# Batch attention with 64x64 value-sum tiles and halved GpSimd products, and a new order on the way into the experts

## The chip, the core and the metric

The kernel runs on one core of a Trainium2 chip. The metric is the device time of one execution in microseconds. The core's engines are PE (TensorE, matmuls; PEld is its weight load), DVE (VectorE), ACT (ScalarE), POOL (GpSimd) and SP (SyncE, which here only issues transfers). Each runs its own instructions in order, and they wait for each other on semaphores.

## The reference, cut to what matters

The program is a chain of eight layers on x (8 samples, 256 positions, 256 features). The change lies in the fourth, `L1_ffn`. It attends over the samples of one position, not over positions, and then sends each token to two of eight experts.

```python
qkv = src @ in_proj_w.T + in_proj_b          # src: 256 positions x 8 samples x 256
q, k, v = ...reshape(s_len, bsz, H, dh)      # H = 16 heads, dh = 16
scores = jnp.einsum('sbhd,tbhd->bhst', q, k) * scale
attn = jax.nn.softmax(scores, axis=-1)
ctx = jnp.einsum('bhst,tbhd->sbhd', attn, v).reshape(s_len, bsz, d)
x = _ln(src + ctx @ out_w.T + out_b, ln1_g, ln1_b)
tok = x.reshape(-1, d)
logits = tok @ gate_w.T + gate_b
probs = jax.nn.softmax(logits, axis=-1)
topv, topi = jax.lax.top_k(probs, K)         # K = 2 of E = 8 experts
...
for e in range(E):
    h = jax.nn.relu(tok @ w1[e].T + b1[e]) @ w2[e].T + b2[e]
    moe_out = moe_out + combine[:, e:e + 1] * h
return _ln(x + moe_out, ln2_g, ln2_b)
```

As the layer is called, the eight samples of a position attend to each other: for each position and head an 8x8 table.

## The kernel before, in words

The stage is called samp. Its 16 units are (sample, half of the positions): a unit u has 128 positions on the partitions, one query sample and all eight key samples (B = 8, T = 2 halves, D = 256, DH = 16, P = 128, C = 2 halves of the features). Per unit:

- POOL multiplies the query with the eight keys, 128x2048 products (`product`, line 2286 in an order with d outermost, line 2289 in the plain order).
- The 16 products of a head are summed either on DVE (`ON_DVE`, the reduction of line 2121, from SBUF) or on PE (`ON_PE`, `products_summed`, 16 matmuls with the identity on line 2374, which leaves the sums in PSUM).
- DVE takes the maximum (2125) and subtracts it (2126), ACT takes the exponent (2330), DVE sums, inverts and scales (2131, 2132, 2133: `probs`).
- DVE multiplies the values in PSUM with the shares (2140, `values`), and PE sums over the eight samples while it transposes (`values_summed`, line 2385: 16 matmuls of 128x128 with the identity). ACT copies the sum (2345).
- PE adds the residual and the projection (`projected`, 2408 and 2411); DVE measures mean and variance (2146, 2147, 2151: `measured`), POOL makes the reciprocal root (198, 201: `rstd_of`), DVE scales (2157: `normed`); PE transposes (2393, `turned`), ACT copies (2348), PE makes the gate's logits (2417, `gated`).

All engines step through one loop over `it`. In iteration `it` PE projects unit it-1, turns and gates unit it-3, sums the values of unit `it` and the products of unit it+2; POOL makes the products of unit it+2. In PE's instruction stream one f32 matmul shows as two MATMUL records.

The picks of the two experts are made in five batches of units, (0-3), (4-7), (8-10), (11-13), (14-15). For a batch DVE reads the logits (2164), picks (2176 to 2190), signals `sel_ready`; PE counts the ranks (`ranked`, 2401, 2402); DVE makes the slots (2211 to 2220, `slots`); POOL then scatters the rows of the batch to their places in DRAM (2298, two indirect transfers per unit, in the iterations of the table `SCATTERED`). Where a batch is ranked, PE first runs nine matmuls that compute nothing (`clocked`, line 1908, on bf16, 512 columns).

After the last batch DVE makes the table of groups (`counted`), SP loads the rows of the first group of 128 tokens, and the experts begin (`moe_pe`: 2509 turns the rows, 2520 is the first product, 2530 the second). POOL zeroes a buffer (674) and then asks for the weights of experts 1 and 2 (2485, 2486). Between the last units PE also makes tables of position biases for a later layer in six parts (`bias_products`, line 2097).

In rows, `L2385` is line 2385 of the kernel, and `scr<-PS,W` says what is written and read.

## Time and profile before

| | before |
|---|---|
| median of 3 runs | 1125.13 us (1124.1 to 1125.45) |
| profiled execution, its own time | 1122.43 us |
| its span in the trace | 1120.7 us |
| PE busy / DVE busy / POOL busy, of the span | 94% / 67% / 47% |
| mean granted TensorE clock | 0.986 |

The span runs from the first to the last instruction; the time of the run is 1.7 us longer. Busy shares are averages over stages that have different limits, so a stage is read from its own stretch. The granted clock is a share of 2.4 GHz: 1.0 is 2.4 GHz and 0.5 is 1.2 GHz. The stage samp runs from about 427 to 580 us, and the experts begin at 585.42 us.

### The profile page before, as it was taken

The page shows a single profiled execution, that of the slowest core. Times are in us where ns is not written, and L with a number is a line of the kernel's source. Part 1 is how long each engine was busy: PE and PEld are TensorE (multiplying, and loading weights), DVE is VectorE, ACT ScalarE, POOL GpSimd, SP SyncE. Part 2 cuts the span into 40 slices and gives each one's busy share as a digit, 9 for nine tenths or more (in the row PEclk, how much of TensorE's full clock was granted, in tenths as well). Part 3 has the DMA queues.
Part 4 walks back from the last instruction along what each step waited for, and adds up shares of the span by engine and source line. Part 5 has one row for each costly group of instructions (what it writes and reads, how often), then busy time and mean ns, then how long its engine had stood idle before and what let it go on. Part 6 is the DMA issues. An engine that isn't in the chain of part 4 may idle for free.

```text
span 1120.7 us, 23972 instructions
## 1 busy us (share of the span) xinstructions
PE 1049.6 (94%) x8906; PEld 826.1 (74%) x8906; DVE 748.5 (67%) x1698; ACT 469.1 (42%) x940; POOL 531.8 (47%) x526
## 2 busy tenths in 40 slices
PE   9999889988899999999989999999999999999896
PEld 5676656666676567999868999999998567765564
DVE  4899879999987448889842222222222899987794
ACT  2555677775565202121112222222222446654475
POOL 5645335577873214768764010000354757541464
PEclk9999999999999999999969999999999989999999
DMA  5999900002000300000147141311221200000001
GB/s 186 368 404 389 388 8 2 23 4 91 2 1 2 107 0 1 1 11 29 57 145 304 60 174 46 113 37 37 66 80 38 67 11 11 1 1 1 0 20 57
DMA packets 45137, 93.78 MB, mean 84 GB/s; under 512 B 3934, under 2 KB 19071, under 8 KB 42487
## 3 DMA queue, kind: packets, MB, share of 16 engines
q1 hardware_dynamic: 36646, 62.24, 15.7%
q0 software_dynamic: 7104, 29.14, 7.2%
q8 instruction: 59, 0.97, 0.3%
q10 hardware_dynamic: 1296, 1.18, 0.3%
q14 instruction: 32, 0.25, 0.1%
HBM read 39.02 MB, written 51.51 MB: 81 GB/s over the span
## 4 chain that ended last, share of the span: by engine, by line
PE 64%; DVE 19%; POOL 5%; ACT 5%; issue 4%; DMA 2%; POOLq 1%; PEldq 0%; DVEq 0%; ACTq 0%; SPq 0%; PEld 0%
PE PS L2520 11%; PE PS L2530 11%; PE PS L1113 4%; PE PS L2029 4%; PE PS L2385 3%; PE PS L1089 3%; PE PS L1126 3%; PE PS L1079 2%; PE PS L1908 2%; PE PS L2374 2%; PE PS L1743 2%; POOL big L695 2%; DVE scr L476 2%; PE PS L1037 1%; PE PS L970 1%
## 5 line engine op out<-in xcount | busy, mean ns | idle before, releaser
L2554 ACT ACTIVATE scr<-PS,W 128x128 f32<-128x128 f32 x148 | 53.5, 367 | 191.1 <-PE PS L2520 191.1
L2520 PEld LDWEIGHTS PS<-scr 128*128 128x128 f32 x992 | 116.5, 192 | 5.5 <-issue 1.8
L2520 PE MATMUL PS<-scr 128*128 128x128 f32 x992 | 118.7, 276 | 1.9 <-issue 1.5
L2530 PE MATMUL PS<-scr 128*128 128x256 f32 x496 | 112.2, 379 | 0.0
L2585 DVE TENSOR_SCALAR scr<-PS,W 128x128 f32<-128x128 f32 x148 | 51.2, 350 | 88.0 <-PE PS L2520 88.0
L727 POOL TENSOR_TENSOR scr<-scr,small 128x1232 f32<-128x1232 f32 x32 | 72.0, 2250 | 73.1 <-DVE small L478 73.0
L2591 DVE TENSOR_TENSOR scr<-PS,W 128x256 f32<-128x256 f32 x37 | 15.7, 425 | 127.0 <-PE PS L2530 123.1
L2530 PEld LDWEIGHTS PS<-scr 128*128 128x128 f32 x496 | 91.8, 190 | 11.2
L868 ACT ACTIVATE big<-PS 128x512 f32<-128x512 f32 x144 | 73.0, 523 | 58.7 <-PE PS L1089 58.1
L2631 POOL DMA_DIRECT2D expert_out<-scr x28 | 15.2, 544 | 161.4 <-DVE scr L2591 159.5
L1089 PE MATMUL PS<-W,scr 128*128 128x128 f32 x480 | 78.6, 284 | 9.4 <-ACT big L846 3.0
L1089 PEld LDWEIGHTS PS<-W,scr 128*128 128x128 f32 x480 | 52.2, 141 | 23.9 <-ACT big L846 4.6
L2385 PE MATMUL PS<-W,scr 128*128 128x128 f32 x512 | 61.1, 278 | 2.4 <-DVE scr L2140 2.4
L1113 PEld LDWEIGHTS PS<-scr,big 128*64 128x64 f32 x1280 | 45.2, 137 | 22.0 <-issue 20.5
L2385 PEld LDWEIGHTS PS<-W,scr 128*128 128x128 f32 x512 | 58.5, 192 | 3.4 <-DVE scr L2140 3.3
L863 ACT ACTIVATE scr<-scr 128x1232 f32<-128x1232 f32 x48 | 58.7, 1223 | 4.3 <-POOL scr L727 2.7
L1908 PE MATMUL PS<-identb 128*128 128x512 bf16 x225 | 58.5, 402 | 0.3 <-ACT big L868 0.3
L1113 PE MATMUL PS<-scr,big 128*64 128x34 f32 (+1 forms) x1280 | 56.7, 228 | 1.1 <-ACT big L868 0.9
L1126 PE MATMUL PS<-W,big 128*128 128x256 f32 x192 | 55.3, 410 | 0.5 <-ACT big L889 0.5
L695 POOL TENSOR_TENSOR big<-big,neghalf 128x32 f32<-128x32 f32 x8 | 45.5, 5687 | 15.9 <-DVE big L431 15.7
L1743 PE MATMUL PS<-big,W 64*64 64x256 f32 x768 | 47.0, 382 | 1.3 <-ACT scr L1662 1.3
L478 DVE TENSOR_REDUCE small<-scr 128x16 f32<-128x1232 f32 x32 | 45.9, 1436 | 1.1
(432 smaller groups left out, 2424.1 us busy)
## 6 DMA issues: line engine op xcount, KB each, us to landing
expert_in<-zeros SPq DMA_DIRECT2D x1, 19712.0 KB, 59.9
expert_out<-zeros SPq DMA_DIRECT2D x1, 19712.0 KB, 112.4
scr<-ew_in POOLq DMA_DIRECT2D x12, 1024.0 KB, 6.4
scr<-expert_in SPq DMA_DIRECT2D x38, 128.0 KB, 2.1
big<-ew_in POOLq DMA_DIRECT2D x4, 1024.0 KB, 8.5
expert_out<-scr POOLq DMA_DIRECT2D x28, 128.0 KB, 2.0
W<-pack SPq DMA_DIRECT2D x1, 2458.0 KB, 8.6
W<-pack SPq DMA_DIRECT2D x1, 2152.0 KB, 9.1
```

What stands on the lines that cost most here:

```text
L695: g.tensor_tensor(a_qr[j % 2], a_qvar[j % 2], neghalf[:, 0:T * H], ALU.pow).then_inc(s["qr_ready"], 1)
L727: g.tensor_tensor(sc3, sc3, a_mx[u % 3].unsqueeze(2).broadcast_to([P, H, S2]), ALU.subtract).then_inc(s["sub_ready"], 1)
L863: a.activation(a_sc[lay][u % 3], a_sc[lay][u % 3], ACT.Exp, scale=scale).then_inc(s["p_ready"], 1)
L868: a.activation(a_PT[lay][u % 2][:, 4 * g:4 * g + n, :], bank(ring_bank(lay, "p", u, g), n * P).rearrange("p (c n) -> p c n", c=n), ACT.Cop ...
L1089: ins = pe.transpose(bank(b, P, k * P), a_sc[lay][u % 3][:, at:at + P], ident)
L1113: ins = pe.matmul(PS[k:k + OUT_COLS, 6 + u % 2, at:at + n * (DH + 1)], a_PT[lay][u % 2][:, c, k:k + OUT_COLS], a_VB[lay][:, c, 0:n, u // T ...
L1126: ins = pe.matmul(bank(6 + u % 2, D, D), a_OT[lay][:, c, :], wo[:, c, :], start=(c == 0), stop=(c == C - 1))
L1743: ins = pe.matmul(PS[c * HALF:(c + 1) * HALF, conv_bank(i, p, r), 0:S], f_taps[rows, f, j, rows], f_G[rows, f, j:j + S], start=(j == 0), s ...
L1908: pe.matmul(bank(b, size, at), identb[:, :], identb[:, :].unsqueeze(1).broadcast_to([P, size // P, P]), start=True, stop=True)
L2385: ins = pe.matmul(bank(4, P, c * P), vp[:, t, c * P:(c + 1) * P], ident, start=(t == 0), stop=(t == B - 1))
L2520: ins = pe.matmul(bank(1 + f % 4, G), e_w1[slot][:, k, f * P:(f + 1) * P], e_xT[:, k, :], start=(k == 0), stop=(k == C - 1))
L2530: ins = pe.matmul(bank(5 + t, D), e_h[:, f, t * P:(t + 1) * P], e_w2[slot][:, f, :], start=(f == 0), stop=(f == FC - 1))
```

## The change

- Three more units (6, 10, 14) have their products summed on PE: `ON_PE` was the odd units from 3 on, and is now all from 3 on but 4, 8 and 12. Their sums go to bank 7 instead of 5.
- For units in `ON_PE` POOL makes the products in two halves by d, and PE starts on the first eight while the second half is made.
- `values_summed` uses 64x64 tiles: each 128x128 matmul becomes four of 64 rows, 64 weight columns and 64 moving columns; the row halves go to two banks.
- PE waits for ACT's copy of the value sum (`cT_ready`) ahead of `clocked` and `turned`, and adds the residual (`based`) ahead of that wait.
- The end of the loop, iterations 16 to 19, is written out: picks before `measured`, ranks and bias parts interleaved anew, 40 instead of 20 matmuls of `clocked` before the experts.
- SP and no longer POOL asks for expert 0's weights, and PE and ACT read the group table ahead of turning the first rows.

```diff
-        ON_PE = [u for u in range(UNITS) if u % 2 and u > 2]
+        ON_PE = [u for u in range(UNITS) if u % 4 and u > 2]
...
+            normed(UNITS - 2)
+            v.wait_ge(s["y_full"], UNITS)
+            logits_read(LAST_BATCH - 1, False)
+            picked(LAST_BATCH - 1)
+            measured(UNITS - 1)
+            v.wait_ge(s["y_full"], UNITS + 1)
+            slots(LAST_BATCH - 1, True)
+            normed(UNITS - 1)
+            shared(LAST_BATCH - 1)
...
-                    g.tensor_tensor(by_d, q.rearrange("p t (h d) -> p t h d", h=H), k.rearrange("p t (h d) -> p t h d", h=H),
-                                    ALU.mult).then_inc(s["prod_ready"], 1)
+                    q4, k4 = (m.rearrange("p t (h d) -> p t h d", h=H) for m in (q, k))
+                    for ds in (slice(0, DH // 2), slice(DH // 2, DH)):
+                        g.tensor_tensor(by_d[:, :, :, ds], q4[:, :, :, ds], k4[:, :, :, ds], ALU.mult).then_inc(s["prod_ready"], 1)
...
-                if it == UNITS:
-                    g.wait_ge(s["b_pe"], len(ON_PE))
-                    g.wait_ge(s["b_dve"], len(ON_DVE))
-                    weights_load(g, 0, 0)
...
+                    if d == DH // 2:
+                        pe.wait_ge(s["prod_ready"], u + turns(ON_PE, u))
...
-                        ins = pe.matmul(bank(4, P, c * P), vp[:, t, c * P:(c + 1) * P], ident, start=(t == 0), stop=(t == B - 1))
+                        for r in range(2):
+                            rows = slice(r * half, (r + 1) * half)
+                            for k in range(2):
+                                at = c * P + k * half
+                                ins = pe.matmul(PS[k * half:(k + 1) * half, SUM_BANKS[r], SUM_AT + c * half:SUM_AT + (c + 1) * half],
+                                                vp[rows, t, at:at + half], ident[rows, rows], start=(t == 0), stop=(t == B - 1))
...
+            turned(UNITS - 2)
+            bias_products(pe, 2, BIAS_BANKS[2])
+            gated(UNITS - 2)
+            ranked(LAST_BATCH - 1).then_inc(s["y_full"], 1)
+            bias_products(pe, 3, BIAS_BANKS[3])
+            turned(UNITS - 1)
+            gated(UNITS - 1).then_inc(s["y_full"], 1)
+            bias_products(pe, 4, BIAS_BANKS[4])
+            pe.wait_ge(s["y_taken"], turns(TAKES, UNITS))
+            ranked(LAST_BATCH).then_inc(s["y_full"], 1)
+            bias_products(pe, 5, BIAS_BANKS[5])
             pe.sem_inc(moe["xT_psum"], 1)
-            clocked(pe, 4, 20)
+            clocked(pe, 4, 40)
...
+            sp.wait_ge(samp["b_pe"], len(ON_PE))
+            sp.wait_ge(samp["b_dve"], len(ON_DVE))
+            sp.dma_start(e_slot[0][:, 0:2048], ew1_in[0]).then_inc(in_w2, 16)
+            sp.dma_start(e_slot[0][:, 2048:4096], ew2_in[0]).then_inc(in_w2, 16)
...
-            transpose_rows(0)
             pe.wait_ge(samp["slot_ready"], len(BATCHES) + 1)
-            moe_experts(pe, body)
+            moe_experts(pe, body, begin=transpose_rows)
```

On PE, before, this stands where the first batch is ranked, in iteration 7 (2385: the value sum of unit 6; 1908: `clocked`; 2393: `turned`; 2401, 2402: ranks; 2408, 2411: residual and projection):

```order
L2385 MATMUL PS<-W,scr 128x128 x15
L1908 MATMUL PS<-identb 128x512 [waits samp_xT_ready]
L1908 MATMUL PS<-identb 128x512 x8
L2393 MATMUL PS<-W,big 128x128 [waits samp_xT_ready,samp_x1_ready]
L2393 MATMUL PS<-W,big 128x128
L2401 MATMUL PS<-scr,W 128x32 [waits samp_sel_ready,samp_y_taken]
L2402 MATMUL PS<-scr,W 128x32
L2408 MATMUL PS<-big,W 128x256
L2411 MATMUL PS<-W,scr 128x256 [waits samp_cT_ready]
```

On PE, of the change, the same place (2420: the value sum, now 64 matmuls; 2429: `turned`; 2437, 2438: ranks; 2444, 2448: residual and projection):

```order
L2420 MATMUL PS<-W,scr 64x64 x63
L1908 MATMUL PS<-identb 128x512 [waits samp_xT_ready,samp_cT_ready,samp_y_taken]
L1908 MATMUL PS<-identb 128x512 x8
L2429 MATMUL PS<-W,big 128x128 [waits samp_xT_ready,samp_x1_ready]
L2429 MATMUL PS<-W,big 128x128
L2437 MATMUL PS<-scr,W 128x32 [waits samp_sel_ready]
L2438 MATMUL PS<-scr,W 128x32
L2444 MATMUL PS<-big,W 128x256
L2448 MATMUL PS<-W,scr 128x256 x2
```

The wait for `cT_ready` moved from the projection to ahead of `clocked`. On DVE, before, this is the fourth batch of picks after the last projection (2164: read the logits; 2146, 2147, 2151: `measured` of unit 15; 2176 and on: the picks; 2157: `normed`):

```order
L2164 TENSOR_TENSOR scr<-PS,W 128x24 [waits samp_y_full]
L2146 BN_STATS scr<-PS 128x6 [waits dve_chain]
L2147 BN_AGGR scr<-scr 128x2 [waits dve_chain]
L2151 SCALAR_TENSOR_TENSOR scr<-PS,scr,W 128x256 [waits samp_x1_ready,samp_var_ready]
L2176 MAX scr<-scr 128x8 x3
...
L2190 TENSOR_TENSOR scr<-scr 128x8 [waits dve_chain] x3
L2199 TENSOR_REDUCE scr<-scr 128x3 [waits samp_texp_ready,samp_sel_ready]
...
L2157 SCALAR_TENSOR_TENSOR big<-scr,W 128x256 [waits samp_y_taken,samp_rstd_ready,dve_chain]
L2211 TENSOR_TENSOR scr<-scr,PS 128x48 [waits samp_y_full]
```

On DVE, of the change, the same batch (2167: read the logits; 2179 to 2193: the picks; 2149 to 2154: `measured`; 2214 to 2223: the slots; 2160: `normed`):

```order
L2167 TENSOR_TENSOR scr<-PS,W 128x24 [waits samp_y_full]
L2179 MAX scr<-scr 128x8 [waits dve_chain]
...
L2193 TENSOR_TENSOR scr<-scr 128x8 [waits dve_chain] x3
L2149 BN_STATS scr<-PS 128x6 [waits samp_sel_ready]
L2150 BN_AGGR scr<-scr 128x2 [waits dve_chain]
L2154 SCALAR_TENSOR_TENSOR scr<-PS,scr,W 128x256 [waits samp_x1_ready,samp_var_ready]
L2214 TENSOR_TENSOR scr<-scr,PS 128x48 [waits samp_y_full]
...
L2223 CAST SLOT<-scr 128x6 [waits dve_chain]
L2160 SCALAR_TENSOR_TENSOR big<-scr,W 128x256 [waits samp_y_taken,samp_rstd_ready]
```

`measured` moved behind the picks, and `normed` and the shares behind the slots.

## Rows read from the trace of the kernel before

**Rows 1.** Four stretches: length, busy PE, PEld, DVE, ACT, POOL, clock, DMA share, GB/s.

```profile
441.00:493.50 52.50, 51.98 (x419) 49.26 (x420) 45.28 (x102) 8.92 (x24) 34.80 (x21) 1.00 0.00 1
493.50:541.00 47.50, 45.11 (x356) 42.12 (x354) 43.75 (x84) 5.65 (x17) 41.61 (x26) 1.00 0.08 29
541.00:560.70 19.70, 19.65 (x146) 17.44 (x147) 14.70 (x48) 2.80 (x9) 13.37 (x17) 1.00 0.19 68
560.70:579.80 19.10, 16.11 (x75) 14.43 (x74) 11.45 (x75) 2.88 (x8) 12.67 (x15) 0.56 0.51 187
```

**Rows 2.** PE in order of time, one iteration; start us, us.

```profile
524.43 3.74 PE L2374 MATMUL PS<-scr,W 128*128 128x128 f32 x32
529.89 3.82 PE L2385 MATMUL PS<-W,scr 128*128 128x128 f32 x32
533.54 0.43 PE L2393 MATMUL PS<-W,big 128*128 128x128 f32 x2
```

**Rows 3.** POOL in order of time, around the last products.

```profile
493.58 4.53 POOL L2289 TENSOR_TENSOR scr<-big 128x2048 f32<-128x2048 f32 x1 [1.03 <-DVE big L2157]
...
498.33 0.55 POOL L201 TENSOR_TENSOR scr<-scr,neghalf 128x1 f32<-128x1 f32 x1
...
534.10 1.05 POOL L2298 DMA_INDIRECT expert_in<-big,SLOT  x1 [0.20 <-issue]
536.44 4.55 POOL L2286 TENSOR_TENSOR scr<-big 128x2048 f32<-128x2048 f32 x1
```

**Rows 4.** DVE in order of time, one iteration with a reduction.

```profile
452.29 2.28 DVE L2140 TENSOR_TENSOR scr<-PS,scr 128x2048 f32<-128x2048 f32 x1
454.49 2.28 DVE L2121 TENSOR_REDUCE scr<-scr 128x128 f32<-128x2048 f32 x1
459.73 2.28 DVE L2140 TENSOR_TENSOR scr<-PS,scr 128x2048 f32<-128x2048 f32 x1
```

**Rows 5.** PE's tiled matmuls elsewhere: groups by line, then a row in time.

```profile
L1743 PE MATMUL PS<-big,W 64*64 64x256 f32 x768 | 47.0, 382 | 1.3 <-ACT scr L1662 1.3
...
892.09 0.89 PE L1113 MATMUL PS<-big 128*64 128x51 f32 x24
```

**Rows 6.** DVE in order of time, a short operation that took long.

```profile
538.22 2.92 DVE L2126 TENSOR_TENSOR scr<-scr 128x128 f32<-128x128 f32 x1
```

**Rows 7.** PE and ACT in order of time, where the second batch is ranked.

```profile
515.35 2.10 PE L1908 MATMUL PS<-identb 128*128 128x512 bf16 x9
514.95 0.21 ACT L2357 ACTIVATE scr<-scr 128x8 f32<-128x8 f32 x1 [3.23 <-DVE scr L2180]
515.61 0.38 ACT L2345 ACTIVATE scr<-PS 128x256 f32<-128x256 f32 x1 [0.46 <-PE PS L2385]
```

**Rows 8.** The way into the experts: PE, POOL, and transfers with time to landing.

```profile
560.20 0.51 PE L2417 MATMUL PS<-W,scr 128*128 128x8 f32 x4
564.28 0.59 PE L2401 MATMUL PS<-scr,W 128*128 128x24 f32 x2 [2.37 <-DVE scr L2190]
578.21 7.12 PE L1908 MATMUL PS<-identb 128*128 128x512 bf16 x20
594.73 3.91 PE L2520 MATMUL PS<-scr 128*128 128x128 f32 x32
567.30 1.05 POOL L2298 DMA_INDIRECT expert_in<-big,SLOT  x1 [3.40 <-DVE SLOT L2220]
578.82 0.97 POOL L2298 DMA_INDIRECT expert_in<-big,SLOT  x1 [0.30 <-issue]
586.95 0.57 POOL L2486 DMA_DIRECT2D scr<-ew_in  x1
scr<-ew_in POOLq DMA_DIRECT2D x2, 1024.0 KB, 6.5
```

**Rows 9.** The other long stall of PE, and the clock around it.

```profile
910.80 0.44 PE L1120 MATMUL PS<-W,big 128*128 128x128 f32 x2 [2.13 <-DVE big L486]
912.00:918.50 6.50, 6.50 (x60) 4.52 (x54) 4.77 (x9) 2.10 (x3) 2.76 (x4) 0.53 0.00 0
```

139 lines of the change are left out of this document (82 added, 57 removed).

## The prediction

> **What bounds the kernel now.** I read the windows by stretch first, then PE, DVE and POOL in order of time, then the transfers. From 441.0 to 560.7 us PE is busy for 51.98 + 45.11 + 19.65 = 116.7 of 119.7 us [rows 1]: PE sets the pace. An iteration on PE is a value sum of 3.65 us (529.89 to 533.54), a rest of about 1.9 us (transposes, projection, gate), and for a unit in `ON_PE` a product sum of 3.6 us: 524.43 to 529.89 is 5.46 us for sum and rest [rows 2].
>
> The reader should see how close the other two are. DVE is busy for 103.7 us of the same stretch [rows 1]; an iteration with a reduction takes it 7.44 us without a stall, of which 2.3 us is the reduction [rows 4]. POOL looks idle in the average, but from the product of unit 10 to the end of that of unit 15 it takes 493.58 to 540.99, 47.4 us, and its own work there is a product of 4.55, a root of 0.8 (0.55 at 498.33 and a short operation ahead of it) and two transfers of 1.27 us (1.0 and a gap of 0.3) each, 7.9 us per iteration: 5 x 7.9 + 4.55 = 44.1 us [rows 3]. So PE can give back little there before POOL binds.
>
> After the last projection, which I set at 560.7 us (560.20 + 0.51), the end is a chain of DVE, PE and POOL: ranks after a stall of 2.37 us, first transfer of the fourth batch at 567.30, last one over at 579.79 [rows 8]. Ten transfers in 12.5 us, without a wait for DVE.
>
> **The price of a value sum.** This decides the sign. The trace has no 64x64 matmul with 64 moving columns. 16 matmuls of two records become 64, that is 128 records. From below: line 1743 has four 64x64 tiles with 256 columns, 47.0 us for 768 records, 61 ns each [rows 5]; at a quarter of the columns 15.3 ns, so 2.0 us per unit. From above: line 1113 has two tiles of 64 weight columns side by side; 24 records start within 0.67 us (0.89 less a drain of 0.22), 29 ns each [rows 5], so 3.7 us, what a unit costs now. Its columns are fewer than 64, so columns don't explain 29 ns. A pair starts every 58 ns, and that is half of the 114 ns (3.65 us for 32) between records of 128 weight columns in [rows 2]: it fits a load of 64 weight columns per tile, which four tiles can do at once as two do. I therefore take the lower end, with 0.1 us for going in and out of the tiles: 2.1 us.
>
> The Trainium skill ("TensorE: Matmul & The Clock Gate", section on 56 ns and not 53.3 ns) says that starts of matmuls never come closer than about 25 ns. For four tiles that speaks against me: by it a unit would cost 128 x 25 ns = 3.2 us. Our closest steady rows, 29 ns, can't decide it.
>
> **The sum, step by step.**
>
> a) *To the product of unit 10* (493.58). PE loses 1.55 us per value sum and gains one product sum of 3.6 us; over eight iterations it has 9 us to give. DVE then binds: it loses one reduction (unit 6), 2.3 us [rows 4]. Of its 7.2 us idle in the first stretch [rows 1] some 4 are gaps of 0.04 us between 102 operations, and of the other 3 I take 0.8 as gained, since a new stall comes (below). Step: -3.1 us.
>
> b) *Unit 10 to 15 on POOL.* At best 44.1 for 47.4 us. Halves cost something between nothing and a small operation's 0.2 us each; five of the six products are in halves, 0 to 1.0 us, and I take 0.5. POOL's stalls on DVE shrink by about as much. Step: -0.3 us, bounds -3.3 and +0.7.
>
> c) *From the last product to the last projection*, 19.7 us. PE starts on the first half early (1.8 us less behind the product), and two value sums give 3.1. But DVE has 14.70 us of work there and two more handovers [rows 1]; I take 16.2 us. Step: -3.5 us.
>
> d) *To the slots of the fourth batch.* `measured` (1.1 us) goes behind the picks, and PE signals after the ranks, with one gate's product less between. Before, 6.3 us from projection to transfer's cause (560.7 to 567.0); now 4.6. Step: -1.7 us. POOL must be free: since its last product it has twelve transfers and four roots, 15.2 + 3.3 = 18.5 us, and the slots come 16.2 + 4.6 = 20.8 us after it. It is. Behind them stand ten transfers, 12.8 us, so the last batch's slots have 7.6 us of cover.
>
> e) *Into the experts: 0.* The group table is read earlier (about 1 us on PE), and SP takes over two transfers. But the second group starts at 594.73 when its weights, asked for by POOL at 586.95 and 6.5 us in flight (the median of two), have just come [rows 8]. POOL asks 7.2 us after its last transfer, and nothing here changes that. So the second group stays 14.9 us behind the last transfer, and what the first gains is lost. The 40 fillers are covered as long as they end 24 us after the last projection: PE gets to them some 10 us after it, and nine take 2.10 us at full clock [rows 7], so 40 take 9 us.
>
> Sum: 3.1 + 0.3 + 3.5 + 1.7 = 8.6 us. The profiled execution took 1122.4 us, which would be 1113.8; the median of the runs shown is 2.7 us above it, so I predict **1116.5 us**. A measurement of this kernel tells about 0.2% (2.2 us) from no change.
>
> **The rivals.**
>
> *Issue-bound tiles (18%), the one that ends slower.* If starts come no closer than 29 ns, a value sum costs 3.7 us, the three product sums add 10.8 us to the engine that binds, and steps a to c turn round: +11.6 less 1.7 from d and some 1 of overlap, +9, 1134 us. At 25 ns (3.2 us) it is 10.8 - 16 x 0.45 = +3.6, less 1.7 and 1: about +1, 1126 us. The skill's floor named above is this case. It decides from 3.65 - 10.8/16 = 3.0 us per value sum. For it: no row shows closer steady starts. Against it: the weight load explains these rows as well. I give each half of the 18%.
>
> *DVE is held while POOL multiplies (18%, with the next).* A subtraction of two SBUF operands that takes 0.29 us elsewhere took 2.92 us, and ended just when POOL's product did, 541.14 against 540.99 [rows 6, 3]. PE's pace hid that. With POOL at products for most of an iteration such stalls hit `probs` (line 2133) more often. If half of the fourteen remaining units lose 0.7 us, it is 5 us: 1121. In the other direction, three such subtractions now read PSUM, and a product in halves lets DVE in after 2.3 us. The skill says in "Advanced Engine Details and Errata", GPSIMD details, that the two share an interface and conflict on two SBUF inputs; the row agrees.
>
> *The clock falls inside the loop.* Where a batch is ranked, ACT does the exponents of the picks (514.95) and only then the copy of the value sum (515.61), while PE ran its fillers (515.35) [rows 7]. Now the fillers stand behind the wait for that copy, and the value sum ends 1.5 us sooner: PE idles about 2.4 us at iteration 11 and 1.4 at 7. Behind a stall of 2.37 us the clock went to half [rows 8, 1], and so it did behind one of 2.13 [rows 9]. Half the clock over 3 to 7 us costs 2 to 3 us: 1119.
>
> *Late fillers (7%).* If PE's clock stays at half at the end, where it stood for most of the last stretch (0.56) [rows 1], 20 fillers take 7.12 us and more, 40 over 14 [rows 8]; if PE gets to them at 13 us after the projection, they end near 29 and cost 5: 1121.5.
>
> **How the numbers follow.** Forecast 57% (its own range 1113 to 1119), tiles 18%, held DVE or clock 18%, fillers 7%. The range 1113 to 1126 leaves out the 29 ns case (9%) and gains over 12 us (4%) and some of the edges. Faster by over 0.2%: the forecast, most of held DVE, clock and fillers, 77%. Within: half of the 25 ns case and the edges of the others, 11%. Slower: 12%.
>
> **What would show it.** The value sum's 128 records: under 2.4 us per unit is right, over 3.0 makes the prediction wrong. The product of unit 10 starts near 490, that of unit 15 ends near 537.6, the last projection near 554, the last transfer ends near 571, the second group starts 14.9 us behind it. If short DVE operations of 1 to 4 us stand beside POOL's products at many places, or the granted clock is 0.5 anywhere before 555 us, the second and third rival have a share. If PE's last filler ends later than 578, the fourth.

## The result, and the profile after

The changed kernel takes **1130.35 us** (median of 9 runs, 1125.39 to 1132.54) where the kernel before, run beside it, takes 1125.13: a ratio of 1.0040, 95% interval 1.0024 to 1.0056. It is slower by 0.4%. I had forecast 1116.5 us and given 12% to slower. Its profiled execution took 1125.39 us, with a span of 1123.6, so the trace shows the fastest of the nine; the median lies 5 us above it, with a lower mean clock in most of the slower runs, and no trace of such a run was taken here. Two executions of later kernels stood far above all others (1448.88 us in e3, 2549.33 in c1) and are left out of the medians and ratios below.

The trace of the kernel before is not quite its counterpart: its own time, 1122.43 us, lies below all nine runs of that kernel in this comparison (1124.02 to 1128.52). More on this stands under groups E and F.

First the four stretches of [rows 1] again, now of the changed kernel, with the same columns:

```profile
441.00:493.50 52.50, 48.78 (x1138) 44.59 (x1127) 44.96 (x101) 8.86 (x25) 37.57 (x26) 1.00 0.01 3
493.50:541.00 47.50, 45.28 (x1002) 41.33 (x1003) 41.76 (x105) 6.06 (x19) 42.30 (x34) 0.96 0.09 31
541.00:560.70 19.70, 15.81 (x301) 12.53 (x299) 10.97 (x25) 1.98 (x6) 10.41 (x14) 0.83 0.46 168
560.70:579.80 19.10, 17.74 (x88) 14.80 (x87) 10.50 (x69) 3.30 (x9) 11.69 (x14) 0.64 0.22 77
```

The reader should see the third row. It was 19.65 us of PE at full clock, and now everything is idler there (PE 15.81, DVE 10.97, POOL 10.41) and the clock has fallen to 0.83. Something stopped all three. PE in order of time shows where:

```profile
545.32 0.79 PE L2420 MATMUL PS<-W,scr 64*64 64x64 f32 x35
547.12 0.29 PE L2420 MATMUL PS<-W,scr 64*64 64x64 f32 x2 [1.00 <-issue]
547.85 0.21 PE L2420 MATMUL PS<-W,scr 64*64 64x64 f32 x1 [0.44 <-issue]
548.58 0.34 PE L2420 MATMUL PS<-W,scr 64*64 64x64 f32 x1 [0.52 <-issue]
549.27 0.52 PE L2420 MATMUL PS<-W,scr 64*64 64x64 f32 x5 [0.36 <-issue]
...
551.48 2.38 PE L2420 MATMUL PS<-W,scr 64*64 64x64 f32 x74 [0.23 <-issue]
...
556.60 2.10 PE L2420 MATMUL PS<-W,scr 64*64 64x64 f32 x128
560.37 1.13 PE L2448 MATMUL PS<-W,scr 128*128 128x256 f32 x4 [0.87 <-ACT scr L2368]
561.33 0.51 PE L2455 MATMUL PS<-W,scr 128*128 128x8 f32 x4
```

A value sum is one run of 128 records without a semaphore inside. That of unit 15 (556.60) takes 2.10 us. That of unit 14 takes 8.53 (545.32 to 553.86): from 547.12 on PE gets a handful of matmuls every 0.73 us, and what it waits for is "issue", nothing that the profile knows. Since no matmul of the row waits for a semaphore, it was PE's instructions that came or started late. From 548.5 to 555.5 the granted clock is then 0.51 (the 1.2 GHz level), so the last 74 records (2.38 us) and the residual behind them (1.22 us, where it is 0.60 at full clock) run at half speed.

The way into the experts, PE, POOL and SP's queue in order of time:

```profile
566.61 1.02 POOL L2315 DMA_INDIRECT expert_in<-big,SLOT  x1 [0.64 <-DVE SLOT L2223]
576.20 0.96 POOL L2315 DMA_INDIRECT expert_in<-big,SLOT  x1 [2.23 <-DVE SLOT L2223]
580.00 0.96 POOL L2315 DMA_INDIRECT expert_in<-big,SLOT  x1 [0.30 <-issue]
576.41 10.20 PE L1908 MATMUL PS<-identb 128*128 128x512 bf16 x40
588.29 0.44 PE L2566 MATMUL PS<-W,scr 128*128 128x128 f32 x2 [1.68 <-issue]
589.29 5.46 PE L2580 MATMUL PS<-scr 128*128 128x128 f32 x32 [0.56 <-ACT scr L2608]
596.20 0.44 PE L2566 MATMUL PS<-W,scr 128*128 128x128 f32 x2 [1.45 <-DMA scr<-expert_in]
588.92 8.24 SPq L2552 DMA_DIRECT2D scr<-expert_in  x2
```

The last transfer ends at 580.96 and the second group starts at 599.92, 18.96 us behind it where it was 14.9 [rows 8]. The 40 fillers end at 586.61; then PE reads the group table (1.68 us of "issue") and only at 588.29 turns the first rows. SP may ask for the second group's rows when that is done, at 588.92. By then POOL has asked for the 4 MB of experts 1 and 2 (from 587.93), and those rows need 7.2 us to land.

### The profile page after: what moved, and what is told of

It is laid out like the page before. It is cut to its first block, busy times and chain, and to the rows that moved or that the text cites. A ratio compares the mean times of both kernels' runs of the same rounds, so it can differ in the third digit from the quotient of the medians.

```text
span 1123.6 us, 27285 instructions
## 1 busy us (share of the span) xinstructions
PE 1042.5 (93%) x10558; PEld 815.4 (73%) x10558; DVE 743.2 (66%) x1695; ACT 469.1 (42%) x940; POOL 533.3 (47%) x534
## 3 DMA queue, kind: packets, MB, share of 16 engines
q1 hardware_dynamic: 36934, 64.33, 16.1%
## 4 chain that ended last, share of the span: by engine, by line
PE 63%; DVE 21%; issue 5%; ACT 5%; POOL 4%; DMA 2%; POOLq 1%; PEldq 0%; DVEq 0%; SPq 0%; ACTq 0%; PEld 0%
PE PS L2590 11%; PE PS L2580 11%; PE PS L2029 4%; PE PS L1113 4%; PE PS L1908 3%; PE PS L2404 3%; PE PS L1089 3%; PE PS L2420 2%; PE PS L1126 2%; PE PS L1079 2%; DVE scr L476 2%; PE PS L1743 2%; POOL big L695 2%; DVE scr L423 1%; PE PS L1037 1%
## 5 line engine op out<-in xcount | busy, mean ns | idle before, releaser
L2649 DVE TENSOR_TENSOR scr<-PS,W 128x256 f32<-128x256 f32 x37 | 15.7, 425 | 126.5 <-PE PS L2590 126.5
L2689 POOL DMA_DIRECT2D expert_out<-scr x28 | 15.3, 546 | 166.2 <-DVE scr L2649 163.7
L1089 PE MATMUL PS<-W,scr 128*128 128x128 f32 x480 | 78.3, 284 | 10.1 <-ACT big L846 3.0
L1089 PEld LDWEIGHTS PS<-W,scr 128*128 128x128 f32 x480 | 52.1, 141 | 24.5 <-ACT big L846 4.6
L1908 PE MATMUL PS<-identb 128*128 128x512 bf16 x245 | 62.4, 398 | 2.6 <-issue 2.6
L695 POOL TENSOR_TENSOR big<-big,neghalf 128x32 f32<-128x32 f32 x8 | 45.5, 5688 | 16.4 <-DVE big L431 16.2
L2304 POOL TENSOR_TENSOR scr<-big 128x1024 f32<-128x1024 f32 x20 | 46.7, 2362 | 8.4 <-DVE big L2160 6.3
L2420 PE MATMUL PS<-W,scr 64*64 64x64 f32 x2048 | 37.6, 224 | 8.8 <-issue 4.6
```

What stands on the lines that cost most here:

```text
L695: g.tensor_tensor(a_qr[j % 2], a_qvar[j % 2], neghalf[:, 0:T * H], ALU.pow).then_inc(s["qr_ready"], 1)
L1089: ins = pe.transpose(bank(b, P, k * P), a_sc[lay][u % 3][:, at:at + P], ident)
L1908: pe.matmul(bank(b, size, at), identb[:, :], identb[:, :].unsqueeze(1).broadcast_to([P, size // P, P]), start=True, stop=True)
L2420: ins = pe.matmul(PS[k * half:(k + 1) * half, SUM_BANKS[r], SUM_AT + c * half:SUM_AT + (c + 1) * half], vp[rows, t, at:at + half], ident[r ...
```

## The experiments

Theories at the start: (1) SP's early transfer of expert 0's weights, which runs from 541 to 549.4, keeps PE's instructions waiting; (2) the tiles alone are too many instructions; (3) fillers (the 40 matmuls of `clocked`) and group table stand in front of the first rows. Five groups (B to F) ran, each on one chip beside the kernel before; A is the first comparison. The table shows each kernel's profiled execution and its runs: the value sum of unit 14, the time from the start of the first value sum to the end of the last projection's four matmuls, the time from the end of the last scattered transfer to the second group, and the longest idle time of DVE or ACT, up to 585 us, before a start that the view of waits marks "remote" (with the usual wait in it). "Remote" means that a semaphore's event ended the wait, but that no instruction which gives this event ended shortly before it.

| kernel, group | sum 14 | to last proj. | last transfer to 2nd group | "remote" | median us | ratio to before |
|---|---|---|---|---|---|---|
| before, A | 3.82 | 125.8 | 14.9 | none | 1125.13 | |
| changed, A | 8.53 | 127.4 | 19.0 | none | 1130.35 | 1.0040 |
| e1_pool_weights, B | 2.32 | 120.9 | 19.7 | none | 1122.76 | 0.9995 (0.9972 to 1.0019) |
| e2_whole_tiles, B | 3.82 | 133.8 | 22.6 | none | 1134.78 | 1.0097 (1.0061 to 1.0133) |
| e3_fill20_turn_first, B | 2.24 | 121.4 | 15.3 | none | 1122.71 | 0.9967 (0.9940 to 0.9995) |
| e4_pool_fill20_turn, B | 2.32 | 123.1 | 15.6 | none | 1117.59 | 0.9943 (0.9921 to 0.9965) |
| c1_after_again (changed), C | 8.80 | 128.2 | 20.0 | ACT 4.8 | 1129.64 | 1.0053 (1.0024 to 1.0082) |
| e5_bulk_tiles, C | 8.50 | 128.3 | 15.1 | ACT 4.8 | 1128.12 | 1.0016 (0.9992 to 1.0040) |
| e6_bulk_before, C | 3.82 | 129.6 | 14.9 | DVE 2.3 | 1126.12 | 0.9994 (0.9972 to 1.0016) |
| e7_filler_first, C | 8.74 | 128.7 | 15.3 | ACT 4.8 | 1127.92 | 1.0019 (0.9999 to 1.0040) |
| c2_pool_weights_again (e4), D | 2.31 | 121.4 | 14.8 | none | 1117.06 | 0.9948 (0.9921 to 0.9975) |
| e8_scatter_later, D | 2.10 | 120.6 | 15.1 | none | 1125.72 | 1.0040 (1.0019 to 1.0062) |
| e9_whole_from_14, D | 3.82 | 123.6 | 16.5 | none | 1122.56 | 0.9996 (0.9975 to 1.0017) |
| c3_sp_weights (e3), D | 2.29 | 121.5 | 15.3 | none | 1118.78 | 0.9977 (0.9957 to 0.9997) |
| c4_pool_weights_third (e4), E | 3.69 | 128.7 | 15.0 | DVE 3.5, ACT 7.3 | 1123.71 | 0.9982 (0.9958 to 1.0006) |
| e10_scatter_later_again (e8), E | 2.09 | 123.9 | 14.9 | DVE 7.9, ACT 6.6 | 1127.47 | 1.0024 (0.9995 to 1.0053) |
| e11_whole_from_14_again (e9), E | 3.82 | 126.5 | 14.8 | ACT 6.2 | 1125.09 | 0.9996 (0.9970 to 1.0021) |
| c5_changed_third (changed), E | 8.40 | 127.5 | 21.8 | none | 1128.71 | 1.0015 (0.9999 to 1.0032) |
| e12_changed_scatter_later, F | 2.09 | 124.7 | 16.1 | DVE 6.5, ACT 7.4 | 1135.03 | 1.0091 (1.0077 to 1.0106) |
| e13_scatter_spread, F | 2.09 | 126.6 | 16.6 | ACT 8.8 | 1128.14 | 1.0033 (1.0019 to 1.0048) |

### Group B: the parts of the change

**e1_pool_weights**, all else as changed:

```diff
-            sp.wait_ge(samp["b_pe"], len(ON_PE))
-            sp.wait_ge(samp["b_dve"], len(ON_DVE))
-            sp.dma_start(e_slot[0][:, 0:2048], ew1_in[0]).then_inc(in_w2, 16)
-            sp.dma_start(e_slot[0][:, 2048:4096], ew2_in[0]).then_inc(in_w2, 16)
...
+                if it == UNITS:
+                    g.wait_ge(s["b_pe"], len(ON_PE))
+                    g.wait_ge(s["b_dve"], len(ON_DVE))
+                    weights_load(g, 0, 0)
```

> The changed kernel with one part undone: expert 0's two weight transfers are asked for by POOL in its iteration 16 again, as before, not by SP at 541 us. Theory 1 (the 2 MB of weights keep PE's instruction fetches waiting): in the changed kernel the value sum at 545.32 took 8.53 us while the transfer engines were busy 90 to 99% of the time, no instruction fetch landed from 539.1 to 552.6, and PE's clock went to half from 548.5 to 555.4. Without that transfer the value sum at 545 takes 2.1 us, the last projection lies near 555 and not at 561.8 us; the time falls by 3 to 6 us, 1125 us or less. It may come back in part: the same transfer now starts near 560 and can starve PE or hold the last transfers there. Theory 2 (64x64 tiles alone are too many instructions for the fetches): the value sum at 545 still stalls by more than 2 us, with the last projection near 560; time 1129 to 1131. Theory 3 (the loss is at the entry to the experts): the last projection moves, the time doesn't.

Measured: sum 14 takes 2.32 us, last projection 6.5 us sooner than in the changed kernel, time level with before. It looked like theory 1. But the changed kernel itself did not run on this chip, and the program of e4 was later seen without a stall in group D and with late starts in group E.

**e2_whole_tiles:**

```diff
-                                ins = pe.matmul(PS[k * half:(k + 1) * half, SUM_BANKS[r], SUM_AT + c * half:SUM_AT + (c + 1) * half],
-                                                vp[rows, t, at:at + half], ident[rows, rows], start=(t == 0), stop=(t == B - 1))
+                        ins = pe.matmul(PS[:, SUM_BANKS[0], SUM_AT + c * P:SUM_AT + (c + 1) * P], vp[:, t, c * P:(c + 1) * P], ident,
+                                        start=(t == 0), stop=(t == B - 1))
```

> The changed kernel with value sums of 16 matmuls of 128x128 into one bank again, all else as changed (SP's early weights, product halves, more product sums on PE, new order of the tail). Each sum costs 3.65 us and not 2.1, so PE has 16 x 1.55 = 25 us more work in the loop, some 10 of it in its slack; with the three further product sums I expect the loop to be 9 to 12 us longer than in a changed kernel without stalls. Theory 1 and 2 both say that the instruction stalls go (a quarter of the instructions): no value sum above 4.5 us, and no 'issue' gap of 1 us at 462 and 510. Against the changed kernel: 10 us for the tiles less 6 for the stall and 3 for the clock, about 1131 to 1135 us. If stalls stay with whole tiles under SP's transfer, the volume is no part of the cause and it goes to 1140.

Measured: no sum above 3.84 us and no stall; the last projection is 12.4 us later than in e3 (below), whose program differs from this one only in the value sums up to there, and 12.9 later than in e1. The tiles are worth what their price said (2.09 against 3.82 us a sum).

**e3_fill20_turn_first** and **e4_pool_fill20_turn** (the same on e1):

```diff
-            clocked(pe, 4, 40)
+            clocked(pe, 4, 20)
...
+            transpose_rows(0)
             pe.wait_ge(samp["slot_ready"], len(BATCHES) + 1)
-            moe_experts(pe, body, begin=transpose_rows)
+            moe_experts(pe, body)
```

(and the same for `transposed(0)` on ACT.)

> The changed kernel with 20 fillers (as before) and not 40 ahead of the experts, and with the first group's rows turned on PE and copied on ACT ahead of the group table, as before. Theory 3: in the changed kernel the fillers ended at 586.61, 1.3 us after the first rows landed, then 1.68 us of register loads stood ahead of the turning; SP asked for the second group's rows at 588.92, behind 4 MB of weights, and they took 7.23 us and not 2.05. With this edit the turning begins when the rows land, SP's request stands ahead of the weights, and the distance from the last transfer to the second group falls from 18.96 to 15 us: 3 to 4 us off, 1126 us by the median. The value sum at 545 stays at 8.5 us. If the clock stays at half for longer for want of fillers, the first group's 32 matmuls take more than 5.5 us and at most 1 us is gained.

> Both edits together: expert 0's weights on POOL as before, 20 fillers, rows turned ahead of the table. If theories 1 and 3 are both right and independent, the gains add: 3 to 6 us and 3 to 4 us against the changed kernel's 1130, so 1120 to 1124 us, faster than the kernel before. If they are one chain (what is gained early waits for the same thing later), it is no better than the better of the two alone.

Measured: the distance from the last transfer to the second group is 15.3 and 15.6 us, against 19.7 in e1. Theory 3 holds, and e4 against e1 is worth 1122.76 - 1117.59 = 5.2 us; how much of it comes from fewer fillers and how much from turning first was not tried apart. But e3 spoke against theory 1, which I had not expected: it has SP's transfer over sum 14 (asked for at 549.34, sum at 553.5) and that sum took 2.24 us.

### Group C: does a bulk transfer starve PE?

> The changed kernel once more, unaltered, beside the others of this group. It tells whether the value sum of 8.53 us at 545 (PE without instructions while expert 0's weights arrive) comes in every execution, or in some: in the run with 20 fillers and rows turned first, the same transfer ran over the same sum, which took 2.24 us, and a fetch that lies 113 us after the first value sum elsewhere lay 116 after it. Theory 1 holds either way; if the stall is here again, in some 5 to 8 us, it is the rule, and the time lies 5 to 7 us above the kernel with POOL's weights (1122.8). If the sum takes 2.1 to 2.7 us, the stall is a matter of chance, and the median shows how often it comes: at or below 1125 would say seldom.

**e5_bulk_tiles** (on e4) and **e6_bulk_before** (on the kernel before):

```diff
+        aside = nc.dram_tensor("aside", (4, P, 2048), F32, kind="Internal").ap()
+        put_aside = sem("put_aside")
...
         def moe_sp(sp):
+            sp.wait_ge(samp["y_full"], 8)
+            for n in range(4):
+                sp.dma_start(aside[n], (ew1_in, ew2_in)[n % 2][n // 2]).then_inc(put_aside, 16)
+            sp.wait_ge(put_aside, 16 * 4)
```

> The version with POOL's weights, 20 fillers and rows turned first (1117.6 us), and to it an extra load: 4 MB copied aside by SP from the middle of the loop on (when PE has signalled eight projections, near 487 us), for some 10 to 20 us. It leaves nothing out. Theory 1 (bulk transfers starve a PE that runs on 64x64 tiles of instructions): at least one value sum or product sum under the copy stalls by 3 us or more without a wait for another engine, the fetches under it lie 1 to 5 us late, and the clock falls after it; the time rises by 5 to 10 us, to 1123 to 1128. If the stall at 545 in the changed kernel had another cause, this copy costs less than 2 us.

> The kernel before, with the same 4 MB copied aside from the same place (eight projections, near 497 us). It leaves nothing out. There PE fetches instructions once in some 16 us and not in 7. Theory 1 with the volume as its condition: no stall above 1 us under the copy, time within 2 us of the kernel before (1123.6). If bulk transfers starve PE whatever the volume, it stalls here as well and loses 4 us or more, and the tiles are no part of the cause.

Under the copy (from 492.12 on), PE of e5 has one stall of 1.40 us:

```profile
502.30 1.50 PE L2426 MATMUL PS<-W,scr 64*64 64x64 f32 x85 [1.40 <-issue]
```

and PE of e6 has none. So this bulk transfer costs tiled sums 1.4 us, not 6 (it is written to DRAM, not into the core's buffers as SP's weights are, so it is near to them and not the same). And both kernels showed something at the old place, where no bulk transfer runs any more. PE of e5, and DVE of e6, which is the kernel before:

```profile
544.69 0.79 PE L2426 MATMUL PS<-W,scr 64*64 64x64 f32 x34
546.47 0.28 PE L2426 MATMUL PS<-W,scr 64*64 64x64 f32 x2 [0.99 <-issue]
547.91 0.38 PE L2426 MATMUL PS<-W,scr 64*64 64x64 f32 x2 [1.15 <-issue]
...
550.89 2.30 PE L2426 MATMUL PS<-W,scr 64*64 64x64 f32 x74 [0.24 <-issue]
```

```profile
549.53 0.51 PE L2419 MATMUL PS<-W,scr 128*128 128x8 f32 x4
550.19 0.96 POOL L2300 DMA_INDIRECT expert_in<-big,SLOT  x1 [0.30 <-issue]
552.47 0.20 DVE L2213 TENSOR_TENSOR scr<-scr,PS 128x48 f32<-128x48 f32 x1 [2.29 <-remote]
```

Theory 1 is refuted as the cause: e5 has its 8.50 us without SP's weights. In e6 DVE starts 2.4 us after PE's ranks and gate, for which it waits, were done (549.53 + 0.51). The common thing at both places is POOL, which issues six scattered transfers in a row. That this is the cause is a new guess here (theory 5 in the expectations below).

**e7_filler_first** puts the nine fillers of a ranking iteration in front of the wait for `cT_ready`:

```diff
+                if q is not None:
+                    clocked(pe, 6, 9)
                 if it:
                     pe.wait_ge(s["cT_ready"], u + 1)
                 if q is not None:
                     pe.wait_ge(s["xT_ready"], x)
-                    clocked(pe, 5, 9)
```

> The version with POOL's weights, 20 fillers and rows turned first (1117.6 us), and to it the nine fillers of a ranking iteration in front of PE's wait for ACT's copy of the value sum, not behind it. Theory: PE idles 1 to 1.4 us there at iterations 7 and 11 and the fillers' 2.1 us (2.94 at half clock) come on top; with the fillers in the idle time each of four iterations gives back 1 to 1.4 us as far as PE sets the pace there, 2 to 4 us in all, 1114 to 1116. Rival: DVE's chain sets the pace in those iterations, and nothing moves (within 1 us of 1117.6).

Behind its fillers, at 480.12 instead of 480.43, PE waits longer for DVE. The rows are of e7 and of c1_after_again:

```profile
484.36 0.41 PE L2433 MATMUL PS<-W,big 128*128 128x128 f32 x2 [2.13 <-DVE big L2160]
```

```profile
483.36 0.44 PE L2429 MATMUL PS<-W,big 128*128 128x128 f32 x2 [0.83 <-DVE big L2160]
```

The rival was right: DVE's chain sets the pace there, and the step gives nothing. In time it stands level with e5 (1127.92 and 1128.12 us); the kernel it was made from did not run in this group.

### Group D: a chip on which nothing stalls

> The version with POOL's weights, 20 fillers and rows turned first, unaltered, as the measure for this group. On the first chip its value sum of unit 14 took 2.32 us and it took 1117.6 us; on the second, two kernels with the same PE program and no transfer of weights at that place took 8.50 and 8.74 us for that sum. So theory 1 (expert 0's weights starve PE) has lost its main witness. New theory 5: at that place PE's instructions come late because POOL issues six scattered transfers in a row there (from 542.7 to 550.1), and how late differs by chip. By it the sum of unit 14 takes either 2.1 to 2.7 us (time 1117 to 1119) or 6 to 9 us (1123 to 1127), and the other kernels of this group tell which part matters.

**e8_scatter_later** and **e9_whole_from_14:**

```diff
-        SCATTERED = {8: (0,), 9: (1,), 10: (2,), 11: (3,), 12: (4,), 13: (5, 6, 7), 14: (8,), 15: (9, 10), 17: (11, 12, 13), 19: (14, 15)}
+        SCATTERED = {8: (0,), 9: (1,), 10: (2,), 11: (3,), 12: (4,), 13: (), 14: (), 15: (5, 6, 7, 8, 9, 10), 17: (11, 12, 13), 19: (14, 15)}
```

```diff
+                        if u >= UNITS - 2:
+                            ins = pe.matmul(PS[:, SUM_BANKS[0], SUM_AT + c * P:SUM_AT + (c + 1) * P], vp[:, t, c * P:(c + 1) * P], ident,
+                                            start=(t == 0), stop=(t == B - 1))
+                            continue
```

> That version with POOL's seven scattered transfers pairs of iterations 13 and 14 (units 5 to 8) held back to iteration 15, so that POOL issues nothing while the value sum of unit 14 runs; it leaves nothing out. Theory 5: where the kernel above takes 6 us or more for the sum of unit 14, this one takes 2.1 to 2.7 there, and a stall may show a few us later, under the row of twelve transfers; its end is up to 8 x 1.27 = 10 us later on POOL, so the total can be slower all the same (1122 to 1130). Rival 6 (the stall belongs to a place in PE's instructions, whatever the others do): the sum of unit 14 takes just as long as in the kernel above.

> That version with the value sums of units 14 and 15 in 16 matmuls of 128x128 and the other fourteen in 64x64 tiles; it leaves nothing out. It costs PE 1.6 us each on paper, 3.2 us, of which I expect 1.5 to 3 to show. Theory 2 (the volume of instructions is a condition of the stall): where the kernel above stalls for 6 us in the sum of unit 14, this one takes 3.8 to 4.5 us, the clock stays at full there, and it is faster than the one above by 3 to 5 us; where that one doesn't stall, this one is slower by 1.5 to 3 us. If the volume is no condition, the stall of 4 us or more stays, in these sums or beside them.

> The version with SP's early weights, 20 fillers and rows turned first (the kernel of the run called e3_fill20_turn_first) beside the same with POOL's weights. Before they stood at 1122.9 and 1117.6 us on one chip. Theory 1, in the weaker form that is left (the early transfer makes a late fetch later): slower than the one with POOL's weights by 3 to 6 us, with a sum of unit 14 or 15 longer than there. If the two are within 1 us, who asks for expert 0's weights and when is no part of the loss, and the earlier 5.3 us were scatter between runs.

Here no start was late, with six transfers in a row as everywhere. POOL and PE of c2_pool_weights_again:

```profile
543.67 0.96 POOL L2315 DMA_INDIRECT expert_in<-big,SLOT  x1 [0.30 <-issue]
544.94 0.96 POOL L2315 DMA_INDIRECT expert_in<-big,SLOT  x1 [0.30 <-issue]
545.14 2.31 PE L2424 MATMUL PS<-W,scr 64*64 64x64 f32 x128
546.20 0.96 POOL L2315 DMA_INDIRECT expert_in<-big,SLOT  x1 [0.30 <-issue]
550.75 2.13 PE L2424 MATMUL PS<-W,scr 64*64 64x64 f32 x128 [0.53 <-DVE scr L2143]
...
568.78 0.96 POOL L2315 DMA_INDIRECT expert_in<-big,SLOT  x1 [1.00 <-DVE SLOT L2223]
572.57 0.96 POOL L2315 DMA_INDIRECT expert_in<-big,SLOT  x1 [0.30 <-issue]
...
588.33 3.83 PE L2577 MATMUL PS<-scr 128*128 128x128 f32 x32
```

Without stalls e8 and e9 show only their costs, 8.7 and 5.5 us; e9's is more than the 1.5 to 3 expected, and no run says why. SP's weights cost 1.7 us by the medians; by the ratios 0.29% here and 0.24% in group B, some 3 us. The profile of this group shows 1.2 of it at the second group, counted from the first value sum (sum 15 takes 2.76 us for 2.13); that of group B shows nothing of it.

### Groups E and F: what the late starts follow

> The version with POOL's weights, 20 fillers and rows turned first, unaltered, as the measure of this group. If the chip is one with the stall: the sum of unit 14 takes 8 to 9 us, the time is 1123 to 1127. If not: 2.3 us and 1117.

> The same with the scattered transfers of units 5 to 8 held back from iterations 13 and 14 to 15; nothing is left out. On a chip with the stall, theory 5 (POOL's row of scattered transfers holds the instructions back): the sum of unit 14 takes 2.1 to 2.7 us. Rival 6 (the stall belongs to that place in PE's instructions): it takes 8 to 9 us. On a chip without it: 2.1 us and 1125.7, as before.

> The same with whole 128x128 tiles in the sums of units 14 and 15; nothing is left out. On a chip with the stall, theory 2: the sum of unit 14 takes 3.8 to 4.5 us and the time is 3 to 5 us below that of the measure. If the volume is no condition, 4 us or more are lost there all the same. On a chip without the stall: 3.82 us and 1122.6, as before.

> The changed kernel, unaltered. On a chip with the stall: 1130 to 1132, 0.4 to 0.5% above the kernel before. On a chip without it I expect it 1 to 3 us above the kernel with POOL's weights and 40 fillers (1122.8 on such a chip): 1123.5 to 1126, within 0.2% of the kernel before or just slower, with the last projection 121 to 122 us after the first value sum and the second group 18 to 20 us behind the last transfer.

> The changed kernel with one edit: the scattered transfers of units 5 to 8 held back from iterations 13 and 14 to 15. It leaves nothing out. The changed kernel has had 8.53, 8.80 and 8.40 us for the sum of unit 14 in three executions, under SP's weights and POOL's row of six. Theory 5 (the scattered transfers hold the instructions back): 2.1 to 2.8 us for that sum, the last projection 120 to 124 us after the first value sum and not 127.5, and the total not better, since POOL has eight transfers, 10 us, still to issue. Theory 1 (SP's weights do it): 6 us or more for that sum. If this is a chip on which nothing stalls, the other kernel of the group shows it by no start above 1 us late.

> The version with POOL's weights, 20 fillers and rows turned first, with the scattered transfers of units 5 to 9 spread out: 5 in iteration 13, 6 in 14, 7 and 8 in 15, 9 in 16, 10 to 13 in 17. It leaves nothing out. If the row of six transfers matters: sums of units 14 and 15 within 0.7 us of 2.1 on any chip, and the same time on POOL's part of the tail plus up to 2 units, 5 us. On a chip that stalls that is 1119 to 1124 and less than 1123.7; on one that doesn't, 1118 to 1122. If any scattered transfer does it, late starts of 2 us and more are still there on a chip that stalls.

The edit of e12 is that of e8 on the changed kernel. That of e13, on e4:

```diff
+        SCATTERED = {8: (0,), 9: (1,), 10: (2,), 11: (3,), 12: (4,), 13: (5,), 14: (6,), 15: (7, 8), 16: (9,), 17: (10, 11, 12, 13), 19: (14, 15)}
```

In c4, with the six transfers from 542 to 549.4, DVE and ACT start late, and PE stalls only a little:

```profile
548.52 0.87 PE L2424 MATMUL PS<-W,scr 64*64 64x64 f32 x29
549.79 0.21 PE L2424 MATMUL PS<-W,scr 64*64 64x64 f32 x1 [0.39 <-issue]
550.52 0.20 DVE L2214 TENSOR_TENSOR scr<-scr,PS 128x48 f32<-128x48 f32 x1 [3.51 <-remote]
561.97 0.38 ACT L2372 ACTIVATE scr<-PS 128x256 f32<-128x256 f32 x1 [7.28 <-remote]
```

In e12 (changed kernel, transfers held back) POOL issues none from its last product to 551.11, and then twelve:

```profile
543.93 2.10 PE L2420 MATMUL PS<-W,scr 64*64 64x64 f32 x128
551.11 1.27 POOL L2315 DMA_INDIRECT expert_in<-big,SLOT  x1 [0.18 <-issue]
552.41 0.35 PE L2420 MATMUL PS<-W,scr 64*64 64x64 f32 x5 [0.41 <-issue]
555.57 0.38 ACT L2368 ACTIVATE scr<-PS 128x256 f32<-128x256 f32 x1 [7.36 <-remote]
559.92 0.39 ACT L2352 ACTIVATE scr<-PS 128x256 f32<-128x256 f32 x1 [3.69 <-remote]
561.65 0.60 PE L2438 MATMUL PS<-scr,W 128*128 128x24 f32 x2
562.08 3.65 PE L2100 MATMUL PS<-zeros,W 128*128 128x64 f32 x16
565.36 0.96 POOL L2315 DMA_INDIRECT expert_in<-big,SLOT  x1 [0.30 <-issue]
568.50 0.20 DVE L2214 TENSOR_TENSOR scr<-scr,PS 128x48 f32<-128x48 f32 x1 [6.52 <-remote]
```

```profile
541.00:545.00 4.00, 4.00 (x92) 3.54 (x93) 3.42 (x8) 0.70 (x2) 0.00 (x0) 1.00 0.93 379
```

The windows row is the test of theory 1 in the changed kernel itself: SP's weights fill the transfer engines (0.93) and sum 14 takes 2.09 us. The late starts have gone with the transfers: PE's sum is done at 552.76, and ACT copies it at 555.57, 2.8 us later. In e10 it is the same: POOL's row starts at 560.03, PE's sum is done at 561.63, ACT starts at 563.72. In e13 the longest row is four transfers, 553.79 to 558.83, and under it ACT comes 4.2 us late (559.66 for a sum done at 555.42). Pairs in earlier iterations held nobody up in e13, but a pair can do it too: in e7 POOL issues two from 498.04 on, and ACT copies a sum that was done at 498.22 only 2.0 us later:

```profile
500.21 0.39 ACT L2372 ACTIVATE scr<-PS 128x256 f32<-128x256 f32 x1 [4.61 <-remote]
```

PE had its product sum to do meanwhile, so this one cost nothing. e11 says what the tiles have to do with it: with whole tiles sum 14 is not stretched, but ACT's copy starts 2.4 us after the sum (552.34 for 549.90), PE waits 2.44 for it, and nothing is won. So the number of instructions seems to decide only whether PE is hit inside a sum (6.4 us in the changed kernel) or an engine beside it (2 to 4 us).

Several expectations of these two groups failed. c4's sum took 3.69 us and not 8 to 9; e11 was not 3 to 5 us faster than c4 but 1.4 slower; c5 stood 0.15% above before and not 0.4 to 0.5%; e13 took 1128.14 us, not less than 1123.7, with a sum 15 of 3.24. And c4 and c5, on one chip, leave theory 1 a share: 3.69 us without SP's weights over the row of six, 8.40 with them. On C's chip they made no such difference (8.80 with, 8.50 and 8.74 without).

**Late signals.** The traces also keep the moment of every semaphore event, and it says what kind of lateness a "remote" start is. Usually the event comes 0.01 to 0.05 us after the end of its instruction. In e12 PE ends the ranks at 562.25 and goes on to the bias part (562.08 in the rows above: matmuls overlap), but the event of the ranks is dated 568.47, and DVE starts 0.03 us behind it. In c4 the gate that DVE waits for ends at 548.59, PE is in the next sum (548.52), and the event is dated 550.49 for DVE's start at 550.52. In e6 it is 550.04, 552.45 and 552.47. So DVE and ACT started at once when the event came; the event was late. In the changed kernel ACT's copy of the last sum is of this kind too (sum done at 558.70, event 559.85, copy 559.93).

The same records tell the two kinds of group apart. On the semaphore of the scattered rows, 48 indirect transfers (the 32 scattered ones and 16 that fetch rows back behind the experts) give 16 events each when they land, 768 in all. The traces of groups B and D have all 768; those of the changed kernel in group A and of groups C, E and F have 355 to 432 of them. The trace of the kernel before has 765. So it is of the kind without late starts and the changed kernel's trace of the other, and a comparison of these two traces counts that difference along with the change. Whether the missing events are lost on the chip or only for the record, and whether keeping the record has a part in the late starts, no run shows.

## Why the prediction was wrong

**What bounds the kernel** was read rightly up to 541 us. **The price of a value sum** was right: 2.09 us in nearly all sums of every trace, predicted 2.1. The starts of 128 records in 2.1 us are 16 ns apart, so the first rival is dead; e2 prices the tiles at 12.4 us up to the last projection. The Trainium skill ("TensorE: Matmul & The Clock Gate", section on 56 ns and not 53.3 ns) says that starts never come closer than about 25 ns. Between four tiles in turn this case measures 16.

**Steps a and b** were right in sign and 1.4 us too large together. The product of unit 10 starts at 491.39 (predicted 490.5), that of unit 15 ends at 539.04 (537.6). Two sums of 3.21 us, stretched by "issue" of 0.8 us (460.6 and 508.9, only with tiles: e2 has none), are part of it; a product in halves costs 4.67 us for 4.55.

**Step c is the step that failed**, and not by its size. "I take 16.2 us": without the late starts it is 16.1 us (c2_pool_weights_again: product 15 ends at 538.81, last gate at 554.89), in the changed kernel 22.8 (539.04 to 561.84). The 6.6 us over the term (6.7 over c2) are sum 14 with its stall and its half clock, 6.2 more than in c2, and 1.1 behind sum 15, whose event is late, less 0.6 that c2 loses between the two sums. The term assumed that an engine starts when its cause is done. [Rows 3] show the pairs of scattered transfers that I counted as POOL's time alone; I did not ask what a row of six does to the others. The trace of before could not have told me: it shows no late start, although e6, the same loop in group C, has one.

**Step d:** the slots of the fourth batch came 4.8 us after the projection, predicted 4.6. "7.6 us of cover" failed: the ten transfers took 14.35 us for 12.5, with 2.23 of waiting for the last batch, because the clock was half from 565.6 to 579.3 and bias part 4 (3.65 us at that clock) stands ahead of the last ranks. With POOL's weights and no stall that wait is 1.00, only because POOL comes to the row later: PE's last ranks end 12.3 us behind the last gate in both.

**Step e, "0", failed by 4.1 us.** I checked that 40 fillers end 24 us after the projection, and they did (586.61 - 561.84 = 24.8, at my bound). I said that the group table is read earlier, but not that it now stands between the fillers and the first rows, and that SP's request for the second rows then falls behind the weights of experts 1 and 2. e4 against e1 shows it: 15.6 for 19.7 us. The rule was in my own text, for weights; it had to be applied to the rows as well.

**The rivals:** held DVE was not needed to explain anything. The clock did fall in the loop, as its rival said (half from 514.4 to 517.8, once), and late fillers had their share in e; I had given the clock an end of 1119 (18% with held DVE) and the fillers 1121.5 (7%), and neither reaches 1130. The mechanism that decides was in no rival.

Adding up for the profiled execution at the second group: 1.4 (a, b) + 6.6 (c) + 1.9 (d) + 4.1 (e) = 14.0 us worse than predicted, so +5.4 us and not -8.6; the traces show 599.92 - 594.73 = 5.19. The end is 2.9 later; 2.3 us differ in the stages behind, where nothing was changed, and I leave them as scatter. These sums go by the trace of before, which has no late starts; e6, the same loop on a chip that has them, is level with it up to sum 14 and reaches its last projection 3.8 us later (129.6 for 125.8), so part of the 6.6 us would fall on the kernel before as well.

Where step e is mended and no start is late, e4 and c2 give -0.57% and -0.52%, about 6 us: the changed kernel with expert 0's weights on POOL, 20 fillers, and the first rows turned ahead of the table. On a chip with late starts (c4) the same program is 0.18% ahead, within the noise, and 5.0 us below the changed kernel (c5). By these ratios the late starts cost it some 4 us against the kernel before.

**What stays open.** Which chips are hit: those of groups A, C, E and F were, those of B and D never, in 8 profiles (whether A's chip is one of the others isn't known), and the changed kernel was never run on one that is not. Its loss differs too: 1.0040, 1.0053 and 1.0015 in groups A, C and E. Why signals come late beside scattered transfers is not shown. Nor is what holds PE inside a sum: no matmul there waits for a signal, but neither does a block of instructions land before PE goes on. The instruction queue has a packet at 539.1 and the next at 552.6, when the sum is nearly over; in c2 it comes at 547.2, with the sum done at 547.45. So the late packet follows the stall and doesn't end it. And it is open what makes the median of the changed kernel 5 us slower than its profiled run.

## What to carry to other kernels

Price a move not only on its engine: ask what each transfer in the row is ahead of, to the last request in the queue, rows and tables too. A gain that depends on engines starting at once needs proof on more than one chip; here one program, alike to 0.8 us in both traces up to the sum of unit 14, reached the last projection 7.3 us later on one chip than on another (c4 and c2). Keep rows of scattered transfers short where other engines set the pace, but do not pay for it with POOL's time at the end: holding back eight of them cost 8.7 us where nothing stalled.

## What the runs showed of the hardware

- 64x64 tiles on four quarters, each with a new weight load and 64 columns: 128 records in 2.09 us, 16 ns each at full clock.
- Instructions are a traffic of their own. The page counts the packets on the instruction queue, of the changed kernel first and then of the kernel before:

```profile
q8 instruction: 72, 1.18, 0.4%
```

```profile
q8 instruction: 59, 0.97, 0.3%
```

Thirteen packets of 16 KB more for 3313 more instructions. The Trainium skill ("Runtime: NRT & Kernel Launch", Instruction fetch mechanics) says that instructions come in blocks of 16 KiB, 256 at a time, fetched ahead and mostly hidden; a value sum in tiles is just 256 (128 loads, 128 matmuls), used up in 2.1 us. The size agrees. "Mostly hidden" may not hold where 4 MB are copied (1.4 us of "issue" in e5), nor in the stretches of 0.8 us in two sums of the changed kernel, the first of them (460.6) at a DMA share of 0.01; that these gaps are waits for instructions is argued, not shown.
- In four of six groups (A, C, E, F) starts on PE, DVE or ACT came 1 to 6 us late while POOL issued scattered transfers, or just behind: mostly rows of four and more, once a pair; in two groups (B, D) never, with the same rows.
- For DVE and ACT these are late semaphore events: dated 1.2 us (the changed kernel, sum 15) to 6.2 us (e12, ranks) after the end of PE's instruction, while PE itself went on (e12 at 562.25, c4 at 548.59, e6 at 550.04); the waiting engine starts 0.02 to 0.08 us after the event.
- Traces with late starts hold 355 to 432 of the 768 landing events of the indirect transfers, those without 765 to 768.
